# Deciding whether to redo a recurrence: a flag loaded beside the last store, and a convergence test taken earlier

## The reference

```
xn = layernorm(x)                                   # x: 8 x 512 x 128
O_lh, O_rh = polar(W_lh), polar(W_rh)               # 12 iterations X <- 1.5 X - 0.5 X X^T X
q = xn Wq;  v = xn Wv
h[0] = identity
h[t+1] = rms(h[t] O_lh^T + q[t] O_rh^T)             # 512 steps in sequence
Y = (h * v) Wc
ffn = sqrt((xn cos(theta+noise))^2 + (xn sin(phi+noise))^2)
out = x + Y + ffn
```

## Time and profile before

| | |
|---|---|
| time, median of 3 runs (lowest, highest) | 129.74 us (129.54, 130.17) |
| the profiled execution, its own time | 129.63 us |
| its span, first to last instruction | 127.5 us |
| granted TensorE clock over the span | 1.000 |
| busy: PE, DVE, ACT, POOL | 91%, 70%, 65%, 53% |
| DMA | 4.94 MB, mean 39 GB/s |

### The profile page before, as it was taken

How to read it: one execution, slowest core, us unless ns; L and a number is a source line. 1 busy time by engine, 2 the same in 40 slices (tenths; PEclk the granted TensorE clock), 3 DMA queues, 4 the chain that set the end, 5 groups by cost and what they waited for, 6 DMA issues and landing times.

```text
span 127.5 us, 2639 instructions
## 1 busy us (share of the span) xinstructions
PE 115.8 (91%) x685; PEld 88.4 (69%) x685; DVE 88.8 (70%) x387; ACT 82.7 (65%) x311; POOL 67.5 (53%) x112
## 2 busy tenths in 40 slices
PE   6999999989998989999999878999999899998761
PEld 6988788879875756767776666776666576776540
DVE  4256778676578776775777726688878788877872
ACT  4145656687268888987889747677677676675410
POOL 6425988776008457200203323868777678886520
PEclk9999999999999999999999999999999999999999
DMA  3884000000000000000000000020202021120211
GB/s 109 272 286 177 8 0 3 0 0 0 5 0 0 0 3 0 0 0 5 0 0 3 0 3 8 0 82 0 82 0 82 3 85 43 39 82 5 82 41 44
DMA packets 3342, 4.94 MB, mean 39 GB/s; under 512 B 448, under 2 KB 1344, under 8 KB 3328
## 3 DMA queue, kind: packets, MB, share of 16 engines
q1 hardware_dynamic: 3024, 4.46, 10.0%
q0 software_dynamic: 160, 0.26, 0.7%
q10 hardware_dynamic: 144, 0.07, 0.2%
HBM read 2.69 MB, written 2.10 MB: 38 GB/s over the span
## 4 chain that ended last, share of the span: by engine, by line
PE 74%; DVE 13%; issue 6%; ACT 4%; POOL 1%; DVEq 0%; ACTq 0%; POOLq 0%
PE bank L1023 9%; PE bank L1003 9%; PE bank L1042 7%; PE bank L910 5%; PE bank L925 5%; PE bank L983 5%; PE bank L992 4%; PE bank L927 4%; PE bank L1043 4%; PE bank L1011 3%; PE bank L862 3%; DVE W L751 3%; PE bank L903 2%; PE bank L1062 2%; DVE SQM L731 2%
## 5 line engine op out<-in xcount | busy, mean ns | idle before, releaser
L327 POOL TENSOR_SCALAR XN<-X,MV,RSTD 128x128 f32<-128x128 f32 x32 | 24.9, 792 | 15.4 <-DVE RSTD L613 15.4
L336 POOL TENSOR_TENSOR FS<-FSQ 128x256 f32<-128x256 f32 x16 | 11.6, 726 | 9.3 <-DVE CROSS L731 9.3
L1003 PE MATMUL bank<-CS,XNT 128*128 128x256 f32 x64 | 16.5, 380 | 0.0
L343 POOL TENSOR_TENSOR XF<-X,FR 128x256 f32<-128x256 f32 x16 | 11.6, 724 | 9.0 <-DVE CROSS L731 9.0
L1023 PE MATMUL bank<-WCT,PV 128*128 128x128 f32 x64 | 14.6, 310 | 1.1 <-POOL PV L371 0.6
L1042 PE MATMUL bank<-PXT,WT 128*128 128x128 f32 x58 | 13.8, 321 | 0.3 <-DVE WT L698 0.2
L751 DVE SCALAR_TENSOR_TENSOR W<-UZ,RT,bank 128x129 f32<-128x129 f32 x30 | 10.5, 350 | 4.1 <-ACT RT L514 3.0
L1042 PEld LDWEIGHTS bank<-PXT,WT 128*128 128x128 f32 x58 | 8.6, 188 | 6.6 <-DVE WT L698 5.4
L1023 PEld LDWEIGHTS bank<-WCT,PV 128*128 128x128 f32 x64 | 9.5, 188 | 5.1 <-issue 1.9
L992 PE MATMUL bank<-MNT,XNT 128*128 128x384 f32 x32 | 13.0, 487 | 0.0
L371 POOL TENSOR_TENSOR PV<-VT,WT 128x128 f32<-128x128 f32 x16 | 7.3, 455 | 10.5 <-issue 9.2
(11 more groups left out here) (182 smaller groups left out, 288.8 us busy)
## 6 DMA issues: line engine op xcount, KB each, us to landing
X<-in_L_attn_x_dram SPq DMA_DIRECT2D x8, 256.0 KB, 6.0
out_dram<-OUT SPq DMA_DIRECT2D x7, 256.0 KB, 2.0
out_dram<-OUT SPq DMA_DIRECT2D x2, 128.0 KB, 2.1
WP<-in_L_attn_W_rh_dram ACTq DMA_DIRECT2D x1, 64.0 KB, 1.9
WP<-in_L_attn_W_lh_dram SPq DMA_DIRECT2D x1, 64.0 KB, 2.1
ANG<-in_L_ffn_theta_dram POOLq DMA_DIRECT2D x1, 64.0 KB, 3.3
WV<-in_L_attn_Wv_dram SPq DMA_DIRECT2D x1, 64.0 KB, 3.1
ANG<-in_L_ffn_phi_dram POOLq DMA_DIRECT2D x1, 64.0 KB, 3.0
```

The lines of the kernel that those rows point to most:

```text
L327: pool.tensor_scalar(XN[:, t, :], X[:, t, :], MV[:, t, 0:1], RSTD[:, t:t + 1], ALU.subtract, ALU.mult).then_inc(S["xn_done"], 1)
L336: pool.tensor_tensor(FS[:, f % 2, :, :], FSQ[:, f % 2, :, 0:P], FSQ[:, f % 2, :, P:2 * P], ALU.add).then_inc(S["ffn_sum"], 1)
L343: pool.tensor_tensor(XF[:, 2 * f:2 * f + 2, :], X[:, 2 * f:2 * f + 2, :], FR[:, f % 2, :, :], ALU.add).then_inc(S["xf_done"], 1)
L1003: last = pe.matmul(FB[:, i * 2 * P:(i + 1) * 2 * P], XNT[:, tile(2 * f + i)], CS[:, :], start=True, stop=True)
```

## The change

Three things. SyncE waits for the flag, loads it and branches right after it has issued the last store; its wait for the stores stands behind the branch (inside it, the redo path has a wait of its own). VectorE's wait for the stores moves into the branch too, to the start of the redo work. And the test is taken apart from the end of the output: on TensorE the product with `DIAG` goes in front of `projected(31)`; on VectorE the subtraction reads the product straight from the bank, with no copy into `EDGE`, and it and the square go in front of `written(31)`. `DIFF` gets the shape of an edge buffer, and its first column per sequence, which the subtraction leaves out, is zeroed at the start of the kernel by one more memset. As the copy counted on `edges`, the waits on `edges` in the redo path go down by one.

```
         DIFF = sb("DIFF", [P, P])                      ->  sb("DIFF", [P, B, NCHUNK])

 SyncE   for first, last in zip((0, *STORES), STORES):
             sp.wait_ge(S["out_done"], last)
             sp.dma_start(out_view[:, first:last, :], OUT[:, first:last, :]).then_inc(S["stored"], 16)
-        sp.wait_ge(S["stored"], 16 * len(STORES))
         sp.wait_ge(S["flag_ready"], 1)
         more = sp.value_load(FLAG[0:1, 0:1], min_val=0, max_val=1)
         with sp.If(more > 0):
+            sp.wait_ge(S["stored"], 16 * len(STORES))
             ...
         sp.end_ifs()
+        sp.wait_ge(S["stored"], 16 * len(STORES))

 VectorE, at the start
+        dve.memset(DIFF[:, :, 0:1], 0.0).then_inc(S["diff_init"], 1)

 VectorE, at the end
-        written(STEPS - 1)
-
         dve.wait_ge(t_done, LAST + 1)
-        dve.tensor_copy(edge_new(EDGE[CHECK % 2]), ends(TB[:, 0:P])).then_inc(S["edges"], 1)
-        dve.wait_ge(S["edges"], 1)
-        dve.tensor_tensor(DIFF[:, :], edge(EDGE[CHECK % 2]), edge(EDGE[(CHECK + 1) % 2]),
+        dve.wait_ge(S["diff_init"], 1)
+        dve.tensor_tensor(edge_new(DIFF), ends(TB[:, 0:P]), edge_new(EDGE[(CHECK + 1) % 2]),
                           ALU.subtract).then_inc(S["diff_done"], 1)
         dve.wait_ge(S["diff_done"], 1)
-        dve.tensor_tensor(DIFF2[:, :], DIFF[:, :], DIFF[:, :], ALU.mult).then_inc(S["diff2_done"], 1)
+        dve.tensor_tensor(DIFF2[:, :], edge(DIFF), edge(DIFF), ALU.mult).then_inc(S["diff2_done"], 1)
+        written(STEPS - 1)
         ...                                            (L823, L826)
-        dve.wait_ge(S["stored"], 16 * len(STORES))     (now at the start of the redo work)

 TensorE
-        projected(STEPS - 1)
-
         pe.wait_ge(wt_ready, LAST + 1)
         pe.wait_ge(diag_ready, CHECK + 1)
         pe.matmul(TB[:, 0:P], W[:, 0:P], DIAG[:, :], start=True, stop=True).then_inc(t_done, 1)
+        projected(STEPS - 1)
```

More of the change, by code:

```diff
@@ L142, in bass_layer @@
         PV = sb("PV", [P, 4, P])
-        DIFF = sb("DIFF", [P, P])
+        DIFF = sb("DIFF", [P, B, NCHUNK])
         DIFF2 = sb("DIFF2", [P, P])
@@ L197, in bass_layer @@
             ang_sum turn_a turn_b turn_c turn_d cs_done
-            ffn_done ffn_sq ffn_sum ffn_root xf_done h0_placed edge_init eps_ready
+            ffn_done ffn_sq ffn_sum ffn_root xf_done h0_placed edge_init diff_init eps_ready
             shift_placed e0_placed size2_done tol_ready
@@ L826, in _ @@
             dve.tensor_scalar(FLAG[:, 0:1], SAME[:, :], P - 0.5, None, ALU.is_lt).then_inc(S["flag_ready"], 1)
-            dve.wait_ge(S["stored"], 16 * len(STORES))
             def end_normalised(n, inverse):
@@ L837, in starts @@
             def starts():
+                dve.wait_ge(S["stored"], 16 * len(STORES))
                 dve.wait_ge(S["rinv_done"], STEPS // 2)
                 end_normalised(1, RINV[:, STEPS - 1:STEPS])
-                dve.wait_ge(S["edges"], 2)
+                dve.wait_ge(S["edges"], 1)
             def again(p, q, odd):
@@ L1092, in again @@
                 if isinstance(q, int) and q == 0 and odd == 0:
-                    pe.wait_ge(S["edges"], p + 1)
+                    pe.wait_ge(S["edges"], p)
                 else:
```

## The result

| | median us | executions (lowest, highest) |
|---|---|---|
| before | 129.85 | 4 (129.54, 130.17) |
| changed | 127.99 | 4 (127.50, 128.17) |
| ratio, 95% interval | 0.9854 | 0.9828 to 0.9881 |

That is 1.9 us (1.55 to 2.2) faster; the forecast was 128.5, with 128.1 as the lower end. It went by a median of 129.74 for the kernel before; a fourth execution makes that 129.85. The profiled execution of the changed kernel took 128.17, with a span of 126.2, and is the longest of its four; that of before took 129.63, near the lowest of the four in the table. So the two traces show less than the medians, 1.46, of which 1.3 lie in the spans.

A forecast was written before the change was run, and what follows sets the result against it. The end was taken as bound by SyncE's and VectorE's load and branch after the last store's landing (126.1 plus 1.2 plus 0.2). Span 127.5 to 126.25, gain 1.25, gave 128.4, or 128.5 on the runs' scale; range 128.1 to 129.0.

The forecast's parts named there:

- One more memset: VectorE at the head: 0.07, hidden by 0.70 of idling for the loaded weights; nothing, or under 0.1 without that cover.
- The sum for the end: Closing strings of store, flag, loads and branches: span ends at 126.25 instead of 127.5, gain 1.25 (1.1 to 1.35).
- The product fits into the idle gap: TensorE before the last projection: product ends at 122.78 to 122.86, inside the gap, costing the projection nothing (0 to 0.1).
- The rival of the missed gap: TensorE takes the product up only at 122.79; store goes 0.42 later, time about 128.8; chance 0.10.
- The difference: VectorE's subtraction reading the bank: priced at 0.28, from a 0.292 row for bank and SBUF operand; ends at 123.16.
- The last row: VectorE's last output row, queued behind difference and square: starts 123.40 against 123.38; store issued about 0.03 later (0 to 0.12).
- the flag: End of the test: flag ready at 124.42 instead of 125.51, 1.09 earlier.
- GpSimd's drain as a fixed cost: At the closing barrier: drain takes 0.486; with the loads moved only, it ends at 127.0, limiting the gain to 0.3.
- The landing: Last store: 1.9 to 2.4 after its output row's end at 123.76, so 125.65 to 126.15; SyncE's drain some 0.05 behind.
- No branch stalled on its code: Rival at the flag's branch: an engine stands still while its target is fetched; 130.3 if TensorE does; chance 0.04.

The follow-up runs named there:

- loads alone: Kernel before, its order kept, with the waits for the stores moved behind the flag's branch (SyncE) and into the redo work (VectorE): 129.43 against 129.63.
- three memsets: Changed kernel with three further spare memsets on VectorE at the head: 127.90, ratio 0.9864 to the kernel before.
- zeroing on GpSimd: Changed kernel with the first column of DIFF zeroed by GpSimd instead of VectorE: 128.31, ratio 0.9894 to the kernel before.
- the halves: Only the store waits moved, in the kernel before: 129.43 against 129.63; changed kernel with the old store waits put back: 128.99 against 129.63.
- memset alone: Kernel before with one more VectorE memset of a spare column at the head and nothing else of the change: 129.21 against 129.63.
- one further memset: Changed kernel with one further spare memset on VectorE at the head: 128.01, ratio 0.9863 to the kernel before.

## Why the prediction was wrong

**The step that failed is the term "One more memset", put at nothing.** Its own 0.07 is hidden, as the earlier trace rows said: the update at 97.59 stands at 97.56 in the changed kernel. What it moves was not asked: every later VectorE instruction stands one place further in the stream, and a stop of 0.4 us that had held up everything from 100.4 on is gone from there; no row of the changed trace shows it elsewhere, so it seems to lie under another wait. Alone it measured 0.43; with 0.43 off, the forecast of 128.5 would have been 128.1, and the runs gave 127.96 and 127.99; the 0.1 that is left is what the end brought over its sum. The sign to look for was in the trace: one step of a loop whose steps take 2.87 took 3.22, behind a root that was long done. I read only the last 5 us of VectorE's list, and the shares of the whole, in which 0.4 us don't show.

**The sum for the end was right in size.** 1.25 with 1.1 to 1.35 as ends, measured 1.37 (1.2 to 1.6) with the stop in its old place. Point by point, in the changed kernel's trace, on the clock of before:

- The product fits into the idle gap and the projection doesn't move: 122.39 and 122.79. The rival of the missed gap is out.
- The difference takes 0.28, the row of the two-operand form. By that row the Trainium skill's dearer PSUM access (Perfetto Trace Analysis, section Optimizing Scalar/DVE Operations) does not show here: the estimate from it was 0.35.
- The last row is 0.04 late (forecast 0.03), the flag 1.08 early (forecast 1.09).
- GpSimd's drain as a fixed cost of 0.49, and as the next one late, holds in three kernels (loads alone, changed, three memsets).
- The landing is where the profiled execution missed: from 123.38 (end of the last row) to 125.9 (SyncE's branch) it is 2.5, and the bound was 2.4; behind the wait stands a branch, not the drain alone, 0.15 and not 0.05. So the span was 126.6 on the clock of before and not 126.15 to 126.4. In two other traces with this end the forecast held: the changed kernel once more took about 2.15 there, with a span of 126.3 on that clock, and the zeroing on GpSimd 2.25, with 126.35. The spans of the six further executions of the changed kernel lay 0 to 0.6 below the profiled one.
- No branch stalled on its code: VectorE takes 1.2 from load to drain, as before, and TensorE's branch, the longest, 0.36 in both. That rival is out. The wait of the Trainium skill's rule on taken branches (Runtime: NRT & Kernel Launch, section Instruction fetch mechanics) shows in no run here, which neither confirms nor refutes the rule.

**The range was too narrow** for the number of things it stood on: below it had 0.2 for the spread of executions and nothing for effects outside the stretch that I had read.

What stays open: what VectorE does during the stop (the runs show that it goes with the place in the stream, not its mechanism), and what spreads executions of one kernel by half a microsecond and more (127.43 to 128.51 with three memsets).

## What to carry to other kernels

Before a change is costed, lay equal steps of a loop side by side: a step that is longer than its siblings, behind a releaser that was long done, may be a loss that an added or removed instruction ahead of it moves, for better or worse, as one memset did here. An end with several strings side by side pays only when all are cut: here the halves brought 0.25 and some 0.2, both together 1.37. And a gain near half a per cent is checked against a kernel in which only the instruction count has changed.

## What the hardware showed unexpectedly

- VectorE stops for 0.33 to 0.41 us at one instruction of its stream (100.4 before), and a fetch on the instruction queue follows: it starts about 0.65 behind the held-up instruction wherever the stop is seen (100.81 and 101.5, 100.86 and 101.5, 123.48 and 124.1). One more or one fewer instruction ahead moves the stop: off the chain (memset alone, 0.43 gained), back (zeroing on GpSimd), onto the last row (one further memset, 0.33), out of sight (three further).
- With such a fetch running beside its data the last store, 128 KB, landed 2.1 to 2.6 us after its issue, in seven traces; with the fetch through before the data, 1.8 and 1.9.
- A flag load beside the store's data took 0.55 to 0.57 us in the changed kernel, on five engines, against 0.46 to 0.54 before.
